# Four graph-attention layers by gathered rows: weights in PSUM, row sums on TensorE, heavy tiles first

## The chip, the cores and the metric

One NeuronCore of a Trainium2 chip runs the whole program. The metric is the device time of one execution in microseconds (us). Below, PE or TensorE is the matmul engine, DVE or VectorE the vector engine, ACT or ScalarE the activation engine, POOL or GpSimd the engine that issues the indirect gathers, and SP the engine that issues most plain DMAs.

## What is computed

The input is `x`, 4096 nodes by 256 features in float32, and `adj`, a symmetric 4096 x 4096 matrix of 0 and 1 with ones on the diagonal (a node has about eight neighbours besides itself, at most 23). Four layers follow each other:

```python
for layer in (L0, L1, L2, L3):
    h = maximum(layernorm(x), 0)
    x = x + layer(h, adj, weights)
```

Layers 0 and 2 are attention with 4 heads: a projection `Wh = h @ W`, a score `leaky_relu(s_i + s_j)` for each pair of neighbours, a softmax over a node's neighbours, and the weighted sum of the neighbours' rows of `Wh` (layer 0 applies ELU to it). Layer 1 has one head, weighs the rows of `h` itself and adds `h @ W`. Layer 3 is attention by dot products of a query with the neighbours' keys, 4 heads of 64, and sums their values.

## The kernel before

The kernel first reads `adj` (the "look"): TensorE packs each column's ones into words, DVE decodes them into a list of at most 23 neighbours per node, and the nodes are sorted by their number of neighbours. Sorted, they form `T = 32` tiles of 128 nodes; in tile `t` no node has more than `KS[t]` neighbours besides itself, from 23 in tile 0 to 3 in tile 31. The sum of `KS` is 276. If the graph doesn't fit, a general path (`Dense`) would run, and it doesn't here.

A layer then runs over the 32 tiles in the order `ORDER`: 31, 29, ..., 1, 0, 2, ..., 30, so that light tiles stand at both ends. For each tile

- POOL (`gp_gather`) issues `KS[t]` indirect gathers, each of which fetches one neighbour's table row for the 128 nodes of the tile from HBM (1 KB, in layer 3 2 KB) into a slot of `s_ring`; SP (`sp_own`) loads the node's own row. `s_ring` has `FLOATS = 28000` floats a partition, and its places are given at build time: `after[n]` says how many tiles of this layer must have been summed (`agg`) before tile n may be written. Gathers of layers 0 to 2 are also held to `PACE = 11` tiles ahead of the projection;
- DVE (`vec_scores`, in layer 3 `vec_dots`) makes the scores, ACT (`act_exp`) the exponentials and their sums, DVE divides (`vec_normal`), multiplies all slots by their weights (`vec_weigh`, L1278) and adds the slots up (`vec_sum`, L1286, a reduction over a strided view). In layer 3 ACT does three of the slots (`act_spare`);
- DVE adds the sum to `s_xs` (`vec_finish`) and takes mean and variance (`vec_stats`). ACT takes the root (`act_root`, L830), DVE the reciprocal and the product with the mean (`vec_norm`), ACT makes the next layer's hidden row (`act_hidden`, L843), TensorE transposes it (`pe_hidden`, L1423), ACT copies it out of PSUM (`act_turned`, L852), TensorE projects it (`pe_project`, L1443 to L1453), and ACT writes the row of the next layer's table (`act_row`) to HBM.

The next layer's first gather waits for every row of that table. In layer 3 there is no next table; POOL instead scatters each finished tile to the output (`gp_home`, L729), seven tiles behind the gathers. All waits are on semaphores that are counted; every engine runs its instructions in the order in which its method emits them:

```python
        if L.n < 3:
            for n in range(T):
                self.pe_hidden(e, L.n + 1, n)
                self.pe_project(e, L.n + 1, n)
```

On DVE the order is weigh n, norm n-1, scores n+1, sum n, finish n, stats n, normal n+1.

## Time and profile before

| | |
|---|---|
| time of a run, median of 3 | 2163.33 us (2163.15 to 2164.61) |
| profiled execution, its span | 2212.0 us |
| DVE busy in it | 1549.9 us (70%) |
| POOL busy | 1372.2 us (62%) |
| ScalarE busy | 811.5 us (37%) |
| TensorE busy with matmuls | 559.5 us (25%), mean granted clock 0.545 of full speed |
| the look and the sorting, before the first gather | 280.6 us |

The span reaches from the first to the last instruction of the profiled execution, a run of its own, which took longer than the three timed ones. Busy time counts an engine's own instructions, without waits and without the issuing of DMAs, save for the indirect ones, which POOL makes itself.

### The profile page before, as it was taken

To read this page: it belongs to the slowest core of one execution; us is meant where nothing else is said; L and a number is where in the kernel's file an instruction comes from. 1 tells how busy PE (TensorE), PEld (TensorE's weight loads), DVE (VectorE), ACT (ScalarE), POOL (GpSimd) and SP (SyncE) were. 2 spreads that over 40 slices of the span, in tenths; PEclk is the share of its full clock that TensorE was granted. 3 is DMA by queue.
4 is the path that set the end of the run, shared out by engine and by line. 5 is a ranking of instruction groups with operands and counts; after the bars stand their busy time and mean duration, and the time that the engine had idled before them with its cause. 6 is when DMAs were issued, how large, how long until landed. Compare 5 with 4: busy or idle time off the path is not lost.

```text
span 2212.0 us, 11389 instructions
## 1 busy us (share of the span) xinstructions
PE 559.5 (25%) x2091; PEld 280.8 (13%) x2092; DVE 1549.9 (70%) x2500; ACT 811.5 (37%) x2030; POOL 1372.2 (62%) x1200
## 2 busy tenths in 40 slices
PE   3565101221223232122343215545552000000000
PEld 2434000110111111011121102212220000000000
DVE  3878423999888677477875327897654987459897
ACT  6877002553456333113343214434443321102233
POOL 0000576788774777878737767887305788547885
PEclk9755555555555555555555556666665555555555
DMA  9996483444442444344425434444205665445663
GB/s 375 405 367 238 167 213 102 116 102 99 107 110 69 133 117 115 102 105 110 113 64 156 118 104 119 127 122 131 78 28 187 198 180 161 132 110 174 187 198 101
DMA packets 171382, 328.55 MB, mean 149 GB/s; under 512 B 40094, under 2 KB 83111, under 8 KB 171304
## 3 DMA queue, kind: packets, MB, share of 16 engines
q0 software_dynamic: 65920, 197.88, 33.1%
q1 hardware_dynamic: 82600, 104.48, 13.9%
q10 hardware_dynamic: 22784, 25.40, 3.3%
q14 instruction: 59, 0.48, 0.1%
q8 instruction: 19, 0.31, 0.1%
HBM read 288.94 MB, written 38.72 MB: 148 GB/s over the span
## 4 chain that ended last, share of the span: by engine, by line
POOL 36%; issue 23%; ACT 12%; DVE 11%; PE 10%; another core or an unknown queue 5%; DMA 2%; ACTq 1%; SPq 1%; POOLq 0%; DVEq 0%
POOL s_ring L722 35%; DVE s_y L1286 5%; PE ps L1443 3%; ACT s_a L768 2%; PE ps L1412 2%; ACT L887 2%; ACT s_pr L887 2%; PE ps L1447 2%; DMA s_ring<-s_tab,s_idx 1%; DVE s_ring L1278 1%; DVE s_sc L1221 1%; DVE s_ring L1219 1%; POOL out_dram L729 1%; ACT s_hb L843 1%
## 5 line engine op out<-in xcount | busy, mean ns | idle before, releaser
L722 POOL DMA_INDIRECT s_ring<-s_tab,s_idx x1104 | 1297.2, 1175 | 571.5 <-issue 334.4
L1286 DVE TENSOR_REDUCE s_y<-s_ring 128x256 f32<-128x2048 f32 (+12 forms) x128 | 566.9, 4429 | 2.4 <-ACT s_ring L907 2.4
L1278 DVE TENSOR_TENSOR s_ring<-s_ring,s_pr 128x1792 f32<-128x1792 f32 (+14 forms) x128 | 323.4, 2526 | 3.4
L887 ACT ACTIVATE s_pr<-s_sc,s_least 128x8 f32<-128x8 f32 (+12 forms) x416 | 124.2, 301 | 413.4 <-DVE s_least L1225 261.1
L1451 PE MATMUL ps<-s_wx,s_hT 128*128 128x258 f32 (+1 forms) x256 | 134.8, 682 | 199.3 <-ACT s_hT L852 104.0
L709 POOL DMA_INDIRECT s_pay<-s_pay_t,s_rank_i x32 | 30.9, 966 | 238.3 <-DVE s_rank_i L1083 228.9
L1219 DVE TENSOR_TENSOR s_ring<-s_ring 128x2304 f32<-128x2304 f32 (+12 forms) x32 | 87.1, 2722 | 114.8 <-DMA s_ring<-s_tab,s_idx 114.7
L1423 PE MATMUL ps<-s_ident,s_hb 128*128 128x128 f32 x128 | 44.1, 448 | 437.7 <-ACT s_hb L843 319.5
L989 DVE RECIPROCAL s_stat<-s_stat 128x1 f32<-128x1 f32 x96 | 15.2, 159 | 188.4 <-issue 95.5
L830 ACT ACT_TABLE_LOAD x94 | 120.6, 1283 | 63.1 <-issue 35.9
L907 ACT ACTIVATE s_ring<-s_ring,s_pr 128x64 f32<-128x64 f32 x384 | 95.2, 334 | 120.8 <-issue 64.8
L887 ACT ACT_TABLE_LOAD x94 | 120.6, 1283 | 47.5 <-issue 45.2
L1443 PE MATMUL ps<-s_wx,s_hT 128*128 128x512 f32 x128 | 120.5, 1097 | 67.3 <-ACT s_hT L852 46.7
L768 ACT ACTIVATE s_a<-s_adj 128x4096 fp8e4<-128x4096 int32 x32 | 115.4, 3606 | 12.9 <-DMA s_adj<-in_adj_dram 12.9
L869 ACT ACTIVATE s_tb<-ps 128x256 f32<-128x256 f32 x32 | 12.3, 384 | 262.3 <-PE ps L1448 145.2
L1451 PEld LDWEIGHTS ps<-s_wx,s_hT 128*128 128x128 f32 x256 | 75.1, 324 | 237.4 <-ACT s_hT L852 122.4
L1423 PE MATMUL ps<-s_ident,s_tb 128*128 128x128 f32 x64 | 22.0, 448 | 272.2 <-ACT s_tb L843 195.6
L1205 DVE SCALAR_TENSOR_TENSOR s_sc<-s_ring 128x24 f32<-128x24 f32 (+16 forms) x96 | 18.2, 190 | 100.6 <-DMA s_ring<-s_tab,s_idx 100.2
L1221 DVE TENSOR_REDUCE s_sc<-s_ring 128x36 f32<-128x2304 f32 (+12 forms) x32 | 87.0, 2720 | 1.1
L1423 PEld LDWEIGHTS ps<-s_ident,s_hb 128*128 128x128 f32 x128 | 18.6, 204 | 467.5 <-ACT s_hb L843 346.4
L887 ACT ACTIVATION_READ_ACCUMULATOR s_pr<-s_sc,s_least 128x1 f32 x416 | 77.7, 187 | 0.0
L843 ACT ACTIVATE s_hb<-s_xs,s_stat 128x256 f32<-128x256 f32 x64 | 38.4, 600 | 98.8 <-DVE s_stat L991 82.1
(163 smaller groups left out, 1186.7 us busy)
## 6 DMA issues: line engine op xcount, KB each, us to landing
s_adj<-in_adj_dram SPq DMA_DIRECT2D x32, 2048.0 KB, 14.6
s_ring<-s_tab,s_idx POOLq DMA_INDIRECT x1104
s_tab<-s_tb ACTq DMA_DIRECT2D x32, 256.0 KB
s_ring<-s_tab SPq DMA_DIRECT2D x32, 256.0 KB
s_ring<-s_pay SPq DMA_DIRECT2D x32, 132.0 KB
s_tab<-s_tb ACTq DMA_DIRECT2D x32, 132.0 KB
s_ring<-s_tab SPq DMA_DIRECT2D x32, 132.0 KB
s_tab<-s_pay_t ACTq DMA_DIRECT2D x16, 260.0 KB, 6.5
```

The source lines that it names most:

```text
L722: e.indirect_dma_start(g[:, k, 0:L.row], None, self.tab_d[L.n], bass.IndirectOffsetOnAxis(ap=self.idx[:, t, k:k + 1], axis=0)).then_inc(se ...
L768: e.activation(self.a8[:, q % 2], self.adj[:, r], ACT.Copy, saturate=False).then_inc(self.conv)
L830: e.activation(st[:, 9:10], st[:, 8:9], ACT.Sqrt).then_inc(self.rooted)
L887: m = e.activation(p[:, :, h], s[:, :, h], ACT.Exp, bias=self.least[:, j, h:h + 1], scale=-1.0, accum_out=self.total[:, j, h:h + 1])
L907: m = e.activation(v, v, ACT.Copy, scale=p[:, k, h:h + 1])
L1219: e.tensor_tensor(keys, keys, wide(self.query(n), 1, k + 1), ALU.mult).then_inc(self.v)
L1221: e.tensor_reduce(s, keys.rearrange("p k (h d) -> p k h d", h=4), AX, ALU.add).then_inc(self.v)
L1278: e.tensor_tensor(g, g, wide(p[:, a:], 3, L.hd), ALU.mult).then_inc(self.weighed)
L1286: e.tensor_reduce(self.y[:, n % 2, :], g[:, :, v0:v0 + D].rearrange("p k d -> p d k"), AX, ALU.add).then_inc(self.agg)
L1423: x = e.transpose(self.bank(self.turn_bank(n), P * k, P), h[:, P * k:P * k + P], self.ident[:])
L1443: e.matmul(o, self.hT[:, j, k, :], self.wx[:, k, D:3 * D], start=(k == 0), stop=False)
L1451: x = e.matmul(o[:, 0:cols], self.hT[:, j, k, :], self.wx[:, k, 0:cols], start=(k == 0), stop=(k == 1 and l == 1))
```

## The change

- The ring is laid out once for all four layers (`lay_ring`), with 30100 floats; `agg` counts on over the layers. `PACE` goes. A ring place may be reused once seven tiles, or those that overlap it, are summed.
- Layers 0 to 2 take the tiles heavy ones first (`DOWN`), layer 3 in a written order (`MIXED`).
- The softmax weights `p` are written to PSUM (banks 0 and 1) and read there by `vec_normal` and `vec_weigh`; ACT copies layer 3's query to PSUM (`act_asked`), where `vec_dots` reads it. The weights of the three slots that ACT does are kept in SBUF (`few`).
- `vec_sum` goes. `pe_sum` adds the weighed slots up in PSUM by identity matmuls, in two pieces that `vec_weigh` releases one after the other. TensorE takes the transposes and the projection of tile n-1, then the sum of tile n.
- Layer 1 multiplies by the reciprocal of the sum of weights in `vec_finish`, behind the sum.
- `act_root` and `vec_norm` go; `act_scale` makes the reciprocal root as exp(-0.5 ln(variance + eps)) on ACT, and the product with the mean there too. A table set with both functions is loaded ahead of a layer.
- The neighbours' table rows of a tile are put in order while layer 0 runs (`vec_places`, in place of a copy), tables of layers 1 to 3 begin one row later, and POOL could issue some gathers of the first tiles when all rows but the last four tiles' have landed. How many is in `EARLY`, which is empty for all layers: POOL waits for all rows of the table, and then issues the layer's first gather.

The core of the diff:

```diff
-ORDER = tuple(range(T - 1, 0, -2)) + tuple(range(0, T, 2))
+DOWN = tuple(range(T))
+MIXED = (5, 6, 7, 8, 31, 28, 0, 11, 17, 29, 24, 10, 4, 9, 26, 18, 1, 3, 16, 14, 21, 13, 30, 2, 20, 12, 19, 27, 15, 25, 22, 23)
 PAY = 2 * D + 8 + SLOTS
-FLOATS = 28000
-PACE = 11
+FLOATS = 30100
 SPARED = 3
+LATE = 4
+SOON = 1 + P * (T - LATE)
+EARLY = ((), (), (), ())
...
+def lay_ring():
+
+    spans, at = [], 0
+    for L in LAYERS:
+        for t in L.order:
+            size = (KS[t] + 1) * L.slot + (D if L.n == 3 else 0)
             at = 0 if at + size > FLOATS else at
-            past = [k + 1 for k, (a, b) in enumerate(spans) if a < at + size and b > at]
-            self.after.append(max(past + [m - 7, 0]))
-            self.at.append(at)
...
+            self.em, self.few = s2("em", [P, 2, D]), s2("few", [P, 2, SPARED, 4])
+            self.sc = s2("sc", [P, 2, 4 * SLOTS])
...
+    def total_y(self, n):
+        return self.bank(2 + n % 2, 0, D)
...
+        part = lambda a: a[:, 0:k * H].rearrange("p (k h) -> p k h", h=H)
+        return part(self.sc[:, n % 2, :]), part(self.bank(n % 2, 0, 96))
...
+    def gp_gather(self, e, L, n, a, b):
+        t = L.order[n]
         g = self.rows(L, n)
+        early = b < KS[t]
         if L.n == 0:
-            e.wait_ge(self.listed, 4 - t // 8)
-        if L.after[n]:
-            e.wait_ge(self.agg, T * L.n + L.after[n])
-        if L.n < 3 and n > PACE:
-            e.wait_ge(self.projected, T * (L.n + 1) + n - PACE)
-        for k in range(KS[t]):
-            e.indirect_dma_start(g[:, k, 0:L.row], None, self.tab_d[L.n],
+            e.wait_ge(self.listed, t // 8 + 1)
+        if a == 0 and L.after[n]:
+            e.wait_ge(self.agg, L.after[n])
+        table = self.tab_d[L.n][0:SOON, :] if early else self.tab_d[L.n]
+        for k in range(a, b):
+            e.indirect_dma_start(g[:, k, 0:L.row], None, table,
                                  bass.IndirectOffsetOnAxis(ap=self.idx[:, t, k:k + 1], axis=0)).then_inc(self.gat[n % 8], 16)
...
+            for n in range(soon):
+                if L.n == 1:
+                    e.wait_ge(self.sorted, n + 1)
+                self.gp_gather(e, L, n, 0, EARLY[L.n][n])
+            for j in range(4):
+                e.wait_ge(self.tab_out[j], self.stored(L.n, T - 4 + j))
+            if L.n == 1:
+                e.wait_ge(self.sorted, T)
         for n in range(T):
-            self.gp_gather(e, L, n)
+            self.gp_gather(e, L, n, EARLY[L.n][n] if n < soon else 0, KS[L.order[n]])
...
+    def act_scale(self, e, l, n):
+
+        st, a = self.stat[:, 16 * (n % 2):16 * (n % 2) + 16], self.as_
+        e.wait_ge(self.var_ok, self.norms(l, n) + 1)
+        e.activation(st[:, 8:9], st[:, 7:8], ACT.Ln, bias=self.eps[:]).then_inc(self.a)
+        e.wait_ge(self.a, a.up())
+        e.activation(st[:, 10:11], st[:, 8:9], ACT.Exp, scale=-0.5).then_inc(self.a)
+        e.wait_ge(self.a, a.up())
+        e.activation(st[:, 11:12], st[:, 12:13], ACT.Copy, scale=st[:, 10:11]).then_inc(self.a)
+        e.wait_ge(self.a, a.up())
+
+    def act_hidden(self, e, l, n):
+
         st = self.stat[:, 16 * (n % 2):16 * (n % 2) + 16]
-        e.wait_ge(self.var_ok, self.norms(l, n) + 1)
-        e.activation(st[:, 9:10], st[:, 8:9], ACT.Sqrt).then_inc(self.rooted)
-
-    def act_hidden(self, e, l, n):
-
-        st = self.stat[:, 16 * (n % 2):16 * (n % 2) + 16]
-        e.wait_ge(self.normed, self.norms(l, n) + 1)
+        self.act_scale(e, l, n)
...
+    def act_asked(self, e, n):
+
+        L = LAYERS[3]
+        e.wait_ge(self.own_in[n % 8], self.own_landed(L, n))
+        if n > 1:
+            e.wait_ge(self.scored, 3 * T + n - 1)
+        e.activation(self.asked_for(n), self.query(n), ACT.Copy).then_inc(self.asked)
...
+        e.preload_act_table_set("natural_log_exp_and_others")
+        if l == 1:
+            e.wait_ge(self.ruled, 3 + len(set(KS)))
+        if l == 4:
+            self.act_asked(e, 0)
+            self.act_asked(e, 1)
         for n in range(T):
+            if n and l == 1:
+                self.act_below(e, n - 1)
+            self.act_exp(e, L, n)
             if l == 4:
-                self.act_spare(e, n)
-                if n + 1 < T:
-                    self.act_exp(e, L, n + 1)
-                continue
-            if n:
+                if n + 2 < T:
+                    self.act_asked(e, n + 2)
+                if n:
+                    self.act_spare(e, n - 1)
+            elif n:
                 self.act_hidden(e, l, n - 1)
-            if n + 1 < T:
-                self.act_exp(e, L, n + 1)
-            if n:
                 self.act_turned(e, l, n - 1)
-            if l == 1:
-                self.act_below(e, n)
-            if n:
                 self.act_row(e, l, n - 1)
-            self.act_root(e, l, n)
+        if l == 1:
+            self.act_below(e, T - 1)
         if l < 4:
             self.act_hidden(e, l, T - 1)
-            self.act_table(e, l, T - 1)
+            self.act_turned(e, l, T - 1)
+            self.act_row(e, l, T - 1)
+        else:
+            self.act_spare(e, T - 1)
...
-        e.tensor_scalar(st[:, 8:9], st[:, 7:8], EPS, None, ALU.add).then_inc(self.var_ok)
-
-    def vec_norm(self, e, l, n):
-        vs, st = self.vs, self.stat[:, 16 * (n % 2):16 * (n % 2) + 16]
-        e.wait_ge(self.rooted, self.norms(l, n) + 1)
-        e.wait_ge(self.hidden, T * l + n - 1)
-        e.reciprocal(st[:, 10:11], st[:, 9:10]).then_inc(self.v)
-        e.wait_ge(self.v, vs.up())
-        e.scalar_tensor_tensor(st[:, 11:12], st[:, 6:7], -1.0, st[:, 10:11], ALU.mult, ALU.mult).then_inc(self.normed)
+        e.tensor_scalar(st[:, 12:13], st[:, 6:7], -1.0, None, ALU.mult).then_inc(self.var_ok)
...
+    def vec_places(self, e, n):
+
+
+        vs, k = self.vs, KS[n]
+        m = -(-k // 8) * 8
+        found, values, to = self.place[:], self.hits[:, n, 0:m], self.met_at[:, 0:k]
+        e.tensor_copy(self.hits[:, n, 0:k], self.rows(LAYERS[0], n)[:, 0:k, D + 4]).then_inc(self.v)
+        e.wait_ge(self.v, vs.up())
+        for a in range(0, m, 8):
+            if a:
+                e.match_replace(values, found[:, a - 8:a], values, 0.0).then_inc(self.v)
+                e.wait_ge(self.v, vs.up())
+            e.max(found[:, a:a + 8], values).then_inc(self.v)
+            e.wait_ge(self.v, vs.up())
+        e.tensor_scalar(to, found[:, 0:k], 0.0, float(N + 1), ALU.is_gt, ALU.mult).then_inc(self.v)
+        e.wait_ge(self.v, vs.up())
+        c = self.soonest(n)
+        if c:
+            e.tensor_tensor(to, to, found[:, 0:k], ALU.subtract).then_inc(self.v)
+            e.wait_ge(self.v, vs.up())
+            e.tensor_scalar(self.over[:, n, 0:c], to[:, 0:c], float(SOON - 1), 0.0, ALU.subtract, ALU.max).then_inc(self.v)
+            e.wait_ge(self.v, vs.up())
+            e.tensor_scalar(to[:, 0:c], to[:, 0:c], float(SOON - 1), None, ALU.min).then_inc(self.v)
+            e.wait_ge(self.v, vs.up())
+            e.tensor_copy(self.idx[:, n, 0:k], to).then_inc(self.sorted)
+        else:
+            e.tensor_tensor(self.idx[:, n, 0:k], to, found[:, 0:k], ALU.subtract).then_inc(self.sorted)
...
+    def pieces(self, L, n):
+
+        a, b = SPARED if L.n == 3 else 0, KS[L.order[n]] + 1
+        c = (a + b + 1) // 2
+        return [(a, c), (c, b)] if c < b else [(a, b)]
 
     def vec_weigh(self, e, L, n):
 
         H, v0 = L.heads, D if L.n == 3 else 0
-        a = SPARED if L.n == 3 else 0
-        p = self.scores(L, n)[1]
-        g = self.rows(L, n)[:, a:, v0:v0 + D].rearrange("p k (h d) -> p k h d", h=H)
-        e.wait_ge(self.normal, T * L.n + n + 1)
-        e.tensor_tensor(g, g, wide(p[:, a:], 3, L.hd), ALU.mult).then_inc(self.weighed)
-
-    def vec_sum(self, e, L, n):
-
-        v0, g = D if L.n == 3 else 0, self.rows(L, n)
-        e.wait_ge(self.weighed, T * L.n + n + 1)
-        if L.n == 3:
-            e.wait_ge(self.spared, n + 1)
-        e.tensor_reduce(self.y[:, n % 2, :], g[:, :, v0:v0 + D].rearrange("p k d -> p d k"), AX, ALU.add).then_inc(self.agg)
+        p, parts = self.scores(L, n)[1], self.pieces(L, n)
+        if L.n == 1:
+            e.wait_ge(self.p_ok, T + n + 1)
+        else:
+            e.wait_ge(self.normal, self.normals(L, n))
+        for a, b in parts:
+            g = self.rows(L, n)[:, a:b, v0:v0 + D].rearrange("p k (h d) -> p k h d", h=H)
+            e.tensor_tensor(g, g, wide(p[:, a:b], 3, L.hd), ALU.mult).then_inc(self.weighed, 2 // len(parts))
...
+        self.vec_weights(e, LAYERS[l])
         for n in range(T):
+            self.vec_scores(e, L, n)
+            if L.n == 0:
+                self.vec_places(e, n)
+            if L.n == 1:
+                self.vec_mutual(e, n)
+            if n:
+                self.vec_finish(e, L, n - 1)
+                self.vec_stats(e, l, n - 1)
+            if L.n == 0 and n > 1:
+                self.vec_apart(e, n - 2)
+            self.vec_normal(e, L, n)
             self.vec_weigh(e, L, n)
...
+    def pe_sum(self, e, L, n):
+
+        g, y, g0 = self.rows(L, n), self.total_y(n), T * L.n + n
+        v0, b = D if L.n == 3 else 0, KS[L.order[n]] + 1
+        parts = self.pieces(L, n)
+        if g0 > 1:
+            e.wait_ge(self.x_new, g0 - 1)
+        for i, (a, c) in enumerate(parts):
+            e.wait_ge(self.weighed, 2 * g0 + (i + 1) * (2 // len(parts)))
+            for k in range(a, c):
+                x = e.matmul(y, self.ident[:], g[:, k, v0:v0 + D], start=(k == parts[0][0]), stop=(k == b - 1 and L.n < 3))
+        if L.n == 3:
+            e.wait_ge(self.spared, n + 1)
+            for k in range(SPARED):
+                x = e.matmul(y, self.ident[:], g[:, k, v0:v0 + D], start=False, stop=(k == SPARED - 1))
+        x.then_inc(self.agg)
+
     def pe_layer(self, e, L):
+        l = L.n + 1
         if L.n == 2:
             e.wait_ge(self.missed_ok, 1)
-            e.matmul(self.bank(0, 0, 1)[0:1, :], self.missed[:, 0:1], self.ones[:, 0:1], start=True,
+            e.matmul(self.bank(4, 0, 1)[0:1, :], self.missed[:, 0:1], self.ones[:, 0:1], start=True,
                      stop=True).then_inc(self.met_sum)
             e.wait_ge(self.sym_ok, 1)
-        if L.n < 3:
-            for n in range(T):
-                self.pe_hidden(e, L.n + 1, n)
-                self.pe_project(e, L.n + 1, n)
+        for n in range(T):
+            if n and l < 4:
+                self.pe_hidden(e, l, n - 1)
+                self.pe_project(e, l, n - 1)
+            self.pe_sum(e, L, n)
```

## Rows read from the trace of the kernel before

**Rows 1.** The page: busy time of each engine, and the gathers' group.

```profile
PE 559.5 (25%) x2091; PEld 280.8 (13%) x2092; DVE 1549.9 (70%) x2500; ACT 811.5 (37%) x2030; POOL 1372.2 (62%) x1200
...
L722 POOL DMA_INDIRECT s_ring<-s_tab,s_idx x1104 | 1297.2, 1175 | 571.5 <-issue 334.4
```

**Rows 2.** Windows by layer: length; busy PE, PEld, DVE, ACT, POOL; clock, DMA, GB/s.

```profile
280.60:724.80 444.20, 88.81 (x192) 46.85 (x192) 335.95 (x524) 187.40 (x512) 319.61 (x277) 0.50 0.45 114
724.80:1161.50 436.70, 127.79 (x258) 62.82 (x258) 318.32 (x494) 139.24 (x254) 322.73 (x276) 0.50 0.41 109
1161.50:1678.20 516.70, 218.49 (x384) 87.26 (x384) 308.75 (x421) 183.26 (x478) 315.41 (x277) 0.61 0.39 107
1678.20:2212.00 533.80, 0.00 (x0) 0.00 (x0) 408.44 (x288) 136.22 (x640) 379.00 (x308) 0.50 0.57 167
```

**Rows 3.** Timeline of a heavy tile, layer 2: start, length.

```profile
1440.80 6.56 DVE L1278 TENSOR_TENSOR s_ring<-s_ring,s_pr 128x6144 f32<-128x6144 f32 x1
...
1441.37 6.81 POOL L722 DMA_INDIRECT s_ring<-s_tab,s_idx  x1 [0.30 <-issue]
...
1448.21 11.17 DVE L1286 TENSOR_REDUCE s_y<-s_ring 128x256 f32<-128x6144 f32 x1
...
1449.72 0.95 POOL L722 DMA_INDIRECT s_ring<-s_tab,s_idx  x1 [0.30 <-issue]
```

**Rows 4.** Waits in layer 2, 1213 to 1330 us: total, times, longest.

```profile
ACT s_tb L869 <- remote: 85.4, 4, 25.6
```

**Rows 5.** Groups by line: the reduction over a tile's rows.

```profile
L1286 DVE TENSOR_REDUCE s_y<-s_ring 128x256 f32<-128x2048 f32 (+12 forms) x128 | 566.9, 4429 | 2.4 <-ACT s_ring L907 2.4
```

**Rows 6.** Narrow stretches of TensorE's timeline, read for their starts.

```profile
1473.64 1.06 PE L1447 MATMUL ps<-s_wx,s_hT 128*128 128x256 f32 x2
...
1474.07 0.95 PE L1447 MATMUL ps<-s_wx,s_hT 128*128 128x256 f32 x2
...
1455.28 0.59 PE L1447 MATMUL ps<-s_wx,s_hT 128*128 128x256 f32 x2
...
1455.49 0.59 PE L1447 MATMUL ps<-s_wx,s_hT 128*128 128x256 f32 x2
```

**Rows 7.** Timeline of the last tiles of layer 1.

```profile
1149.11 0.42 DVE L1300 TENSOR_TENSOR s_xs<-s_xs,s_y 128x256 f32<-128x256 f32 x1
...
1150.25 0.15 DVE L983 TENSOR_SCALAR s_stat<-s_stat 128x1 f32<-128x1 f32 x1
...
1152.80 0.20 ACT L830 ACTIVATE s_stat<-s_stat 128x1 f32<-128x1 f32 x1 [0.40 <-ACT s_tb L866]
...
1153.43 0.60 ACT L843 ACTIVATE s_hb<-s_xs,s_stat 128x256 f32<-128x256 f32 x1 [0.42 <-DVE s_stat L991]
...
1154.08 0.69 PE L1423 MATMUL ps<-s_ident,s_hb 128*128 128x128 f32 x2 [2.11 <-ACT s_hb L843]
...
1155.24 2.13 PE L1451 MATMUL ps<-s_wx,s_hT 128*128 128x264 f32 x4 [0.47 <-ACT s_hT L852]
...
1157.30 1.24 PE L1453 MATMUL ps<-s_bx,s_ones 1*128 1x264 f32 x2
```

**Rows 8.** Timeline of layer 0, act_below's second operation.

```profile
698.67 0.42 ACT L897 ACTIVATE s_em<-s_em 128x256 f32<-128x256 f32 x1
```

**Rows 9.** Windows of TensorE in layer 2's projections: length, busy, clock.

```profile
1451.20:1454.30 3.10, 3.10 (x4) 0.50 0.44 117
1454.30:1457.80 3.50, 2.00 (x7) 0.99 0.39 103
1457.80:1465.90 8.10, 0.00 (x0) 0.50 0.49 143
1468.80:1474.80 6.00, 5.99 (x9) 0.50 0.51 138
```

**Rows 10.** Chain that ended last, a landing in layer 3: start, length.

```profile
1889.35 4.12 DMA s_ring<-s_tab,s_idx
```

**Rows 11.** The page: loads of ScalarE's tables ahead of the root.

```profile
L830 ACT ACT_TABLE_LOAD x94 | 120.6, 1283 | 63.1 <-issue 35.9
```

More of the change, by code:

```diff
@@ L536, in query, with asked_for @@
         L = LAYERS[3]
-        a = L.at[n] + (KS[ORDER[n]] + 1) * L.slot
+        a = L.at[n] + (KS[L.order[n]] + 1) * L.slot
         return self.ring[:, a:a + D]
+    def asked_for(self, n):
+        return self.bank(4 if n % 2 == 0 else 6, 0, D)
+    def total_y(self, n):
+        return self.bank(2 + n % 2, 0, D)
     def landed(self, L, n):
-        every = lambda c: sum(KS[ORDER[m]] for m in range(c) if m % 8 == n % 8)
-        return 16 * (L.n * every(T) + every(n + 1))
+        every = lambda M, c: sum(KS[M.order[m]] for m in range(c) if m % 8 == n % 8)
+        return 16 * (sum(every(M, T) for M in LAYERS[0:L.n]) + every(L, n + 1))
     def own_landed(self, L, n):
@@ L842, in act_hidden @@
             h = self.hb[:, n % 2, :]
[L843 removed]
+        e.activation(h, self.xs[:, n, :], ACT.Relu, bias=st[:, 11:12], scale=st[:, 10:11]).then_inc(self.hidden)
     def act_turned(self, e, l, n):
@@ L1183, in vec_lists @@
         vs = self.vs
-        for g in (3, 2, 1, 0):
+        for g in range(4):
             part = slice(8 * g, 8 * g + 8)
```

238 lines of the change are left out of this document (122 added, 116 removed).

## Prediction

> **What bounds the kernel now.** I read the page first. VectorE (DVE) is busy 1549.9 us of 2212.0 and GpSimd (POOL) 1372.2 us, of which 1297.2 us are the 1104 indirect gathers of L722 [rows 1]. The two are close, so I cut the trace where each layer's first gather starts: layers 0 to 3 last 444.2, 436.7, 516.7 and 533.8 us behind a beginning of 280.6 us [rows 2]. In no layer is an engine busy all the time: POOL works 72, 74, 61 and 71% of them, DVE 76, 73, 60 and 77%.
>
> Next I looked at single gathers. An undisturbed one takes 0.95 us and 0.30 us pass to the next, so 1.25 us each. Where the weighing multiply L1278 runs, one gather lasts as long as the multiply: 6.81 us beside 6.56 us. The reduction of 11.17 us behind it holds no gather back [rows 3]. Undisturbed, 276 gathers of a layer need 276 x 1.25 = 345 us. Against 1104 x 0.95 = 1049 us, the 1297.2 us [rows 1] hold 248 us of such holds.
>
> The Trainium skill ("SBUF — State Buffer", Who interferes with whom) says that a `tensor_tensor` with two SBUF inputs takes only the shared read interface and was not seen to stall DMA, since descriptor generation needs the write interface. By that page the move of the weights to PSUM would free nothing; the measured 6.81 us speak against it, and I go by them.
>
> Third, the profiled execution is 48.7 us longer than the median of 2163.33 us. In layer 2, four times, ScalarE waited for something unknown, 85.4 us in all [rows 4], between projections that otherwise follow each other evenly. The gathers ran ahead and took up part of that loss. I place the 48.7 us there, so that layer 2 has 468.0 us in a timed run: 280.6 + 444.2 + 436.7 + 468.0 + 533.8 = 2163.3. My sum is made without such a stall, so it stands against the median; made against 2212.0 it would have 48.7 us more.
>
> **The change part by part.**
> *Weights in PSUM.* `p` and layer 3's query are read from PSUM, so the big multiplies have one SBUF input, as has the reduction, which holds nothing [rows 3]. I take the holds as gone. In layer 3 POOL is busy 379.0 us [rows 2]; 276 gathers and 32 scatters, taken as long as a gather, at 0.95 us would be 292.6, so 86 us go. If the hold stays, nothing goes: both ends are kept.
>
> *Sums on TensorE.* L1286 leaves DVE: 566.9 us, 4.43 us a tile [rows 5]. In its place come 276 + 32 = 308 identity matmuls of 256 columns a layer, each as two instructions. Two such are 0.43 us apart at a granted clock of 0.50 and 0.21 us apart at 1.00 [rows 6]: 0.854 or 0.427 us a slot, 263 or 132 us a layer. DVE then has slack everywhere. TensorE is not hidden, because `pe_layer` now puts transposes and projection of tile n-1 before the sum of tile n. That closes a ring: sum n-1, finish and statistics on DVE, scale and hidden on ScalarE, transposes, copy, projection, sum n.
>
> *The ring, from rows.* From L1300's start (1149.11) to L983's end (1150.40) 1.3 us. The three small ScalarE operations that replace root, reciprocal and product are new; each is like L830, 0.20 us and a handoff of 0.04, so 0.7 us. Hidden 0.60 and handoff: 0.65. From the transposes (1154.08) to the projection (1155.24) 1.2 us [rows 7]. With handoffs F = 4.0 us in layers 1 and 2. Layer 0 adds `act_below`, two operations of 0.42 us with handoffs, and a second DVE operation as long [rows 8]: F = 5.4 us. The small three are bounded by nothing (0) and by 0.60 us each, as L843 (+1.1 us); their form is L830's, so I take 0.7. The projection P at the low clock: 2.1 us for layer 0; 3.3 us in layer 1 with the bias (1155.24 to 1158.54) [rows 7]; for layer 3's weights 5.99 us within the stretch and a little behind it, 6.3 [rows 9].
>
> *The clock.* In the projections of layer 2, TensorE worked from 1451.2 at 0.50 and the clock rose at 1454.3, after 3.1 us of work; in the next round it was still low after 6.0 us. With little work behind the rise it was low again from 1457.8 [rows 9]. So I take the low level (1.2 GHz) for the first 4.5 us of each burst of projection and sum, the middle of the two, and 2.4 GHz behind it: a burst is 4.5 + (P + 0.854 s - 4.5)/2 for s slots, and a round, with 0.15 us of drain, is F + 2.4 + P/2 + 0.427 s. That gives 8.8, 8.0 and 9.6 us + 0.427 s in layers 0, 1 and 2. A mean tile (s = 9.6) needs 12.9, 12.1 and 13.7 us; its gathers 8.6 x 1.25 = 10.8 us. The ring is the new bound, not POOL.
>
> The Trainium skill ("TensorE: Matmul & The Clock Gate", HAM oscillation) says that gaps between bursts return the array to half rate, so that every burst starts cold; the trace agrees.
>
> *Heavy tiles first.* The first tiles have gathers longer than a round (23, 14, 13 gathers: 28.8, 17.5, 16.3 us); behind these the rounds count. Layer 0: tiles 0 to 4, 74 gathers, 92.5 us; 5.6 us for landing and scores; 28 rounds from tile 4 on, 28 x 8.8 + 0.427 x 242 = 349.7; the last tile's way to the next layer's first gather, F + P and 3.0 us (1158.54 to 1161.5 [rows 2, 7]), 10.5: 458. Layer 1: 96 gathers 120; 5.6; 26 x 8.0 + 0.427 x 217 = 300.7; 10.3: 437. Layer 2: 62 gathers 77.5; 5.6; 29 x 9.6 + 0.427 x 255 = 387.3; 14.6 with longer copies: 485. The 5.6 is an estimate: 4.1 us from a tile's last gather to its landing [rows 10] and 1.5 us for three short score operations and an exponential. DVE's start in layer 0 falls within the 28.8 us of tile 0's gathers.
>
> *Layer 3.* No projection, so no ring. DVE does about 9 us a tile, TensorE 4.1 to 8.2. POOL is the bound: 345 us of gathers, 25 scatters between them at 0.95 + 0.30, 32 us; then the last tile and its scatter, about 20 us; 5 us for waits on room in the ring of 30100 floats. 402 us, against 533.8.
>
> *Costed at nothing.* `vec_places` (four to eight short operations a tile) and the exponentials run while TensorE sums; if that cover were gone, about 1.3 us a tile in layer 0, 40 us. The wait for all table rows, on POOL ahead of the whole layer, is there before too; `EARLY` is empty, so the sorted lists bring nothing. Table loads (L830: 94 of 1.283 us [rows 11], as many at L887) go; before they stood mostly beside DVE's reduction.
>
> *Sum.* 280.6 + 458 + 437 + 485 + 402 = 2063 us. Layers 0 to 2 together lose 31 us against 1348.9, layer 3 gains 132. I round to **2060 us**, 4.8% less.
>
> **Rivals.**
> *Clock stays low.* If bursts never raise it, the round is F + P + 0.15 + 0.854 s, 7.6, 7.4 and 10.4 us + 0.854 s. All 32 tiles then follow the ring: with 263 us of sums, the first tile's gathers and the way out, layers of about 553, 546 and 646 us, 2430 us in all. Against: the clock rises in bursts of 6 us [rows 9], and these are longer. It decides from 1.25 us a round on: 83 rounds x 1.25 = 103 us, my whole gain. This is the rival on the other side.
> *Clock stays high through the gaps.* Rounds of 6.6, 5.8 and 7.3 us + 0.427 s equal the gathers' pace, layers of about 390, 381 and 409: 1860 us. Against: it fell in the round shown [rows 9], and the gap stays at 3 to 4 us.
> *Gathers still held.* Then layer 3 keeps its 86 us and the first tiles of the others some 45 more: 2190 us, slower. For it speaks that the multiply still writes the ring; against it, that the reduction, with one SBUF input, held nothing. The page's rule above would have the same effect, by another cause.
> *Table loads within the ring.* If logarithm and exponential each load their own table, 2 x 1.283 us [rows 11] x 83 rounds = 213 us: 2275 us. The change preloads a set with both, so this is unlikely.
> *A slower ring.* Each of about ten handoffs 0.05 to 0.1 us dearer gives 0.5 to 1 us a round: 2100 to 2145 us.
>
> **How the numbers follow.** Forecast with its own range (2005 to 2095) 0.63; slower ring 0.16; clock high 0.08; clock low 0.04; gathers held 0.04; table loads 0.03; the change does nothing 0.02. A result under 0.2% (4 us), about what a measurement of this kernel can tell, counts as the same. Faster 0.87, same 0.02, slower 0.11. For 8 in 10 I take the forecast, the slower ring and a part of clock high: 1975 to 2150 us.
>
> **What would show it.** Gathers at 1.25 us also beside L1278's successor; no reduction of 4.4 us on DVE; TensorE about 1000 us busy, its clock changing once per round; in layers 0 to 2 rounds of 12 to 14 us with POOL waiting for the sum; the layers at 458, 437, 485, 402 us. Wrong, if the bursts are cut into pieces too short for the clock, if gathers are late by DMA in layer 3 (it would move about 220 GB/s where it moved 167 [rows 2]), or if ScalarE's order puts an exponential between statistics and hidden.

## The result, and the profile after

The changed kernel takes 2128.99 us (median of 4 runs, 2128.65 to 2130.79), the kernel before 2163.97 beside it (2163.15 to 2166.78). The ratio is 0.984, 95% interval 0.983 to 0.985: 1.6% or 35 us faster, where 103 were forecast. The profiled execution took 2128.94 us, 1.7 of them outside its span of 2127.2, and has no stall of the kind that [rows 4] show, so it stands against the median as it is.

Groups of the page of the changed kernel (line, engine, operation, count, then busy us and mean ns, idle time before):

```profile
PE 1221.5 (57%) x4555; PEld 834.4 (39%) x4556; DVE 991.3 (47%) x2452; ACT 645.3 (30%) x2069; POOL 1113.2 (52%) x1201
...
L746 POOL DMA_INDIRECT s_ring<-s_tab,s_idx x1104 | 1045.9, 947 | 740.9 <-issue 329.9
L1552 PE MATMUL ps<-s_ring,s_ident 128*128 128x256 f32 x2272 | 670.6, 461 | 380.6 <-DVE s_ring L1372 380.6
...
L864 ACT ACTIVATE s_stat<-s_stat,s_eps 128x1 f32<-128x1 f32 x96 | 28.3, 295 | 299.2 <-DVE s_stat L1033 299.2
```

POOL's gathers fell from 1297.2 us to 1045.9, 0.947 us each, so the holds of [rows 1, 3] are gone. DVE fell from 1549.9 to 991.3 us busy. The new work is on PE, busy for 1221.5 us where the prediction said about 1000. Windows from each layer's first gather to the next (first and last us, length, busy us of PE, PEld, DVE, ACT, POOL with instructions, granted clock, DMA share, GB/s):

```profile
283.50:751.50 468.00, 254.94 (x808) 193.41 (x808) 209.31 (x602) 126.86 (x513) 261.76 (x276) 0.74 0.44 110
751.50:1236.70 485.20, 331.12 (x874) 223.59 (x874) 171.80 (x400) 83.27 (x257) 261.28 (x277) 0.68 0.38 99
1236.70:1714.00 477.30, 324.04 (x1000) 188.67 (x1000) 157.75 (x357) 127.32 (x482) 261.49 (x276) 0.82 0.42 116
1714.00:2127.20 413.20, 186.43 (x616) 144.75 (x616) 273.29 (x319) 142.30 (x672) 293.06 (x308) 0.71 0.71 213
```

Against 458, 437, 485 and 402 us of the forecast, layer 1 stands out: 48 us longer, at the lowest clock. Against [rows 2], with layer 2 at 468.0 as in the prediction, layers 0 to 2 lost 24, 49 and 9 us and layer 3 gained 121.

The rounds are best read from TensorE. A round goes from the transposes of one tile to those of the next, and has one sum in it. From the transposes of tile 4 to those of tile 30 there are 26 rounds, with the sums of tiles 5 to 30, in each of layers 0 to 2:

```profile
413.60:734.50 320.90, 196.04 (x607) 147.66 (x607) 156.18 (x468) 101.70 (x416) 163.09 (x172) 0.77 0.35 93
871.20:1216.80 345.60, 256.15 (x659) 171.05 (x659) 124.62 (x314) 66.59 (x208) 170.56 (x181) 0.69 0.34 93
1352.70:1691.60 338.90, 251.09 (x762) 142.75 (x762) 117.43 (x288) 101.96 (x390) 173.50 (x184) 0.85 0.41 117
```

That is 12.34, 13.29 and 13.03 us a round. The forecast's formula gives, at their mean of 8.65 slots, 12.5, 11.7 and 13.3: right in layers 0 and 2, 1.6 us short in layer 1. One round of layer 1 on PE's timeline (start, length, operation, count, idle time before and what ended it), and its stretches as windows:

```profile
1087.52 0.69 PE L1508 MATMUL ps<-s_ident,s_hb 128*128 128x128 f32 x2 [2.97 <-ACT s_hb L882]
1088.68 2.13 PE L1537 MATMUL ps<-s_wx,s_hT 128*128 128x264 f32 x4 [0.47 <-ACT s_hT L891]
1090.74 1.24 PE L1539 MATMUL ps<-s_bx,s_ones 1*128 1x264 f32 x2
1091.92 6.30 PE L1552 MATMUL ps<-s_ring,s_ident 128*128 128x256 f32 x16
1101.18 0.47 PE L1508 MATMUL ps<-s_ident,s_hb 128*128 128x128 f32 x1 [2.96 <-ACT s_hb L882]
```

```profile
1087.50:1092.00 4.50, 4.00 (x9) 2.04 (x9) 1.84 (x6) 0.38 (x1) 2.68 (x3) 0.50 0.44 116
1092.00:1097.20 5.20, 5.20 (x13) 4.13 (x14) 0.00 (x0) 0.79 (x3) 0.00 (x0) 0.50 0.09 32
1097.20:1100.60 3.40, 1.02 (x5) 0.57 (x3) 2.20 (x6) 0.86 (x4) 1.80 (x2) 1.00 0.27 64
```

The idle gap ahead of the transposes is 2.97 us, and the projection ends 4.5 us behind their start, both as forecast. But the clock stands at 0.50 through 9.7 us of burst and rises when the sum is all but done. Over the 26 rounds it rose, where it rose within a burst, 8.4 us (median) behind the first transpose in layer 1 and 5.4 us in layer 0. One instruction in this list is unlike all others: L1539, the bias, `1*128`, over one partition. Layer 0 has no bias. The first experiment tests this.

### The profile page after: what moved, and what is told of

Read it like the earlier page. It is cut to its first block, busy times and chain, and to the rows that moved or that the text cites. A ratio compares the mean times of both kernels' runs of the same rounds, so it can differ in the third digit from the quotient of the medians.

```text
span 2127.2 us, 16493 instructions
## 1 busy us (share of the span) xinstructions
PE 1221.5 (57%) x4555; PEld 834.4 (39%) x4556; DVE 991.3 (47%) x2452; ACT 645.3 (30%) x2069; POOL 1113.2 (52%) x1201
## 4 chain that ended last, share of the span: by engine, by line
PE 47%; POOL 14%; ACT 14%; DVE 10%; issue 8%; DMA 4%; SPq 3%; ACTq 0%; DVEq 0%; POOLq 0%
PE ps L1552 25%; POOL s_ring L746 12%; PE ps L1537 6%; PE ps L1528 5%; PE ps L1508 3%; SPq L596 3%; ACT s_a L801 2%; PE ps L1497 2%; DVE s_stat L1028 2%; PE ps L1533 2%; ACT s_hb L882 2%; PE ps L1539 2%; ACT s_hT L891 2%; DMA s_ring<-s_tab,s_idx 2%; DMA s_adj<-in_adj_dram 1%
## 5 line engine op out<-in xcount | busy, mean ns | idle before, releaser
L746 POOL DMA_INDIRECT s_ring<-s_tab,s_idx x1104 | 1045.9, 947 | 740.9 <-issue 329.9
L1552 PE MATMUL ps<-s_ring,s_ident 128*128 128x256 f32 x2272 | 670.6, 461 | 380.6 <-DVE s_ring L1372 380.6
L1552 PEld LDWEIGHTS ps<-s_ring,s_ident 128*128 128x128 f32 x2272 | 532.7, 239 | 516.7 <-issue 332.5
L1372 DVE TENSOR_TENSOR s_ring<-s_ring,ps 128x1280 f32<-128x1280 f32 (+8 forms) x255 | 330.9, 1339 | 4.5
L926 ACT ACTIVATE ps<-s_sc,s_least 128x9 f32<-128x9 f32 (+12 forms) x416 | 109.6, 264 | 482.4 <-DVE s_least L1273 254.0
L1267 DVE TENSOR_TENSOR s_ring<-s_ring,ps 128x2304 f32<-128x2304 f32 (+12 forms) x32 | 87.1, 2721 | 125.6 <-DMA s_ring<-s_tab,s_idx 125.3
L864 ACT ACTIVATE s_stat<-s_stat,s_eps 128x1 f32<-128x1 f32 x96 | 28.3, 295 | 299.2 <-DVE s_stat L1033 299.2
L954 ACT ACTIVATE s_ring<-s_ring,s_few 128x64 f32<-128x64 f32 x384 | 94.6, 333 | 0.0
L926 ACT ACTIVATION_READ_ACCUMULATOR ps<-s_sc,s_least 128x1 f32 x416 | 77.6, 186 | 0.0
L1497 PE MATMUL ps<-s_wx,s_hT 128*128 128x264 f32 x128 | 67.3, 681 | 17.2 <-ACT s_pay_t L855 16.5
```

The lines of the kernel that those rows point to most:

```text
L746: e.indirect_dma_start(g[:, k, 0:L.row], None, table, bass.IndirectOffsetOnAxis(ap=self.idx[:, t, k:k + 1], axis=0)).then_inc(self.gat[n % ...
L926: m = e.activation(p[:, :, h], s[:, :, h], ACT.Exp, bias=self.least[:, j, h:h + 1], scale=-1.0, accum_out=self.total[:, j, h:h + 1])
L954: m = e.activation(v, v, ACT.Copy, scale=p[:, k, h:h + 1])
L1267: e.tensor_tensor(keys, keys, wide(self.asked_for(n), 1, k + 1), ALU.mult).then_inc(self.v)
L1372: e.tensor_tensor(g, g, wide(p[:, a:b], 3, L.hd), ALU.mult).then_inc(self.weighed, 2 // len(parts))
L1497: x = e.matmul(self.bank(7, 0, cols), self.hT[:, t % 2, k, :], self.wx[:, k, 0:cols], start=(k == 0), stop=(k == 1))
```

## The experiments

All change `after` (the changed kernel) unless said, and the diffs show the core of each edit. Times are medians of four runs. The ratios are to the kernel before, measured beside them on the same chip: 2162.4 us beside e1, e2, e5 and e6, 2162.94 beside e3, e4, e7 and e8; for the other runs it stands with them. Theory A and theory B are the two that each expectation sets against each other.

**Run e1, the bias over 128 partitions.** `bx` gets 128 partitions, with zeros in all but the first (cleared once, in the beginning):

```diff
-            x = e.matmul(o[:, 0:cols], self.ones[0:1, :], self.bx[0:1, 0:cols], start=False, stop=True)
+            x = e.matmul(o[:, 0:cols], self.ones[:], self.bx[:, 0:cols], start=False, stop=True)
```

> The changed kernel, with one thing different in layer 1 (the projections of its tiles, for layer 2's table): the bias is added by a matmul over 128 partitions (ones times a matrix whose rows below the first are zero) where it is a matmul over one partition; same columns, same values, same number of instructions. In the trace of the changed kernel layer 1's rounds average 13.29 us over tiles 5 to 30 at a sum of 0.730 us a slot, layer 0's 0.582. Theory A, the one-partition matmul of 1.1 us in the middle of layer 1's burst keeps the granted clock from rising: with 128 partitions the sums of layer 1 fall to about layer 0's 0.58 us a slot, some 1.3 us a round, so layer 1 lasts about 450 instead of 485.2 us and the whole 2095. Theory B, the clock depends on the time that TensorE is at work or on the idle gap alone: nothing changes, 2129 within 4 us.

Measured: 2062.02 us, ratio 0.953 (0.951 to 0.955). Layer 1, and one of its rounds of the same 16 sum instructions:

```profile
750.10:1169.70 419.60, 260.18 (x874) 198.67 (x874) 172.19 (x400) 83.19 (x257) 261.41 (x276) 0.77 0.43 114
```

```profile
1050.88 0.44 PE L1511 MATMUL ps<-s_ident,s_hb 128*128 128x128 f32 x2 [2.97 <-ACT s_hb L884]
1051.79 2.12 PE L1540 MATMUL ps<-s_wx,s_hT 128*128 128x264 f32 x4 [0.47 <-ACT s_hT L893]
1053.71 1.08 PE L1542 MATMUL ps<-s_bx,s_ones 128*128 128x264 f32 x2
1054.60 3.72 PE L1555 MATMUL ps<-s_ring,s_ident 128*128 128x256 f32 x16
```

The sum takes 3.72 us for 6.30. Layer 1 went from 485.2 to 419.6 us; layers 0 and 2 stayed, 466.7 for 468.0 and 481.4 for 477.3. Theory A holds, more strongly than expected (30 us more): rounds of 11.04 us, the rise 4.5 us (median) behind the first transpose.

**Runs e10 and e11, the same in layer 0.** A matmul of no use behind each projection, over one partition in e10 and over 128 in e11:

```diff
+                if l == 1:
+                    e.matmul(self.bank(2 + (n + 1) % 2, D, D), self.ones[0:1, :], self.wx[0:1, 0, 0:D], start=True, stop=True)
```

> The changed kernel, with a matmul of no use behind each projection of layer 0 (256 columns, into a part of a bank that nothing reads), over one partition, as layer 1's bias is. Layer 0 has no such matmul now and lasts 468.0 us at 0.582 us a slot. Theory A, a one-partition matmul between projection and sum keeps the granted clock from rising: layer 0's rounds become layer 1's 13.29 plus the longer gap of 1.36 us, 14.65 where they are 12.34, some 70 us more; 2200 in all. Theory B, the clock follows the time at work, whatever the rows: the 1.1 us of work at 0.50 costs at most that a round, 0 to 34 us: 2129 to 2163, and the same as its twin over 128 partitions.

> As the run before, but the matmul of no use in layer 0 is over 128 partitions. Theory A: it counts as work, so that the rise comes no later than now and the matmul pays part of itself: 11.04 plus 1.36 us, 12.4 a round, layer 0 at 465 to 485 us and the whole at 2126 to 2146. Theory B: as its twin over one partition.

Measured: 2528.22 and 2470.77 us, beside 2214.16 for the kernel before (2188.92 to 2227.65). On this chip the engines waited for things that the trace calls remote, which means that it has no name for them, in e10 DVE alone for 256.3 us at one line. In layers 0 to 2 the transposes behind the first sum came 76 to 78 us after it, where 3 to 4.3 are usual. So the totals can't be used. The rounds behind can: layers 1 and 2, which the edit leaves alone, have 13.25 and 13.00 us here, for 13.29 and 13.03 in the changed kernel. Layer 0's 26 rounds, in e10 and then e11:

```profile
502.70:881.80 379.10, 254.24 (x658) 170.84 (x658) 155.92 (x468) 101.71 (x416) 122.26 (x129) 0.70 0.24 64
```

```profile
494.60:827.60 333.00, 208.08 (x659) 158.26 (x659) 155.86 (x468) 101.72 (x416) 122.29 (x129) 0.77 0.28 73
```

14.58 us with one partition (14.65 expected), 12.81 with 128 (12.4), 12.34 without either. The same columns cost 2.2 us a round over one partition and 0.5 us over 128; the rise came at 8.0 and 5.6 us. Theory A.

**Run e2, the gap filled.**

```diff
+            if l < 4 and n < T - 1:
+                for _ in range(17 if l == 1 else 11):
+                    e.matmul(self.bank(2 + (n + 1) % 2, D, P), self.ident[:], self.ones[:], start=True, stop=True)
```

> The changed kernel, with matmuls of no use (128 columns, into a part of a PSUM bank that nothing reads) behind each sum of layers 0 to 2, 17 of them in layer 0 and 11 in layers 1 and 2, so that TensorE is at work through the 4.33 us and the 2.97 and 2.90 us in which it now waits for VectorE and ScalarE. Theory A, the low granted clock after each gap is what makes the rounds 12.3, 13.3 and 13.0 us: without gaps it stays at 1.00, a burst costs half, the rounds fall below the pace of the gathers (1.25 us each) and the layers to about 390, 385 and 410 us: 1880 in all. Theory B, the gap isn't what lowers it (it falls for another reason): the added work of 2.4 and 3.7 us at the high clock takes 4.8 and 7.3 us at the low one, 2 to 3 us longer than the gaps, and the kernel is slower, about 2300.

Measured: 1928.96 us, ratio 0.891 (0.888 to 0.894).

```profile
283.60:684.10 400.50, 306.84 (x1862) 271.37 (x1862) 211.11 (x602) 126.99 (x513) 261.78 (x276) 0.91 0.51 129
684.10:1087.60 403.50, 316.83 (x1556) 251.31 (x1556) 172.07 (x400) 83.20 (x257) 260.97 (x276) 0.87 0.45 119
1087.60:1514.60 427.00, 347.61 (x1682) 253.28 (x1682) 158.47 (x357) 127.02 (x482) 261.64 (x276) 0.94 0.47 130
```

Theory A: more work on TensorE, 200 us less. Rounds fell to 10.24, 10.50 and 11.34 us. The run is 49 us slower than the 1880 of theory A: even at the high clock a round takes longer than the gathers of a mean tile, 9.6 us (7.65 of them of 1.25 us). The Trainium skill ("TensorE: Matmul & The Clock Gate", HAM oscillation) says that gaps return the array to half rate; this run, in which they are down to 0.5 us, agrees (clock 0.99 in layer 0's rounds and 1.00 in layer 2's). In layer 1 it was 0.95 in the projections and 0.89 in the sums, so that a gap isn't the only thing.

**Run e8, filler and bias over 128 partitions** (both edits).

> The run with filler matmuls, and the bias of layer 1's projections over 128 partitions. With filler the granted clock was 0.94 and 0.89 in layer 1's projections and sums and 0.99 to 1.00 in layers 0 and 2: its layer 1 lasted 403.5 us. Theory A, the one-partition matmul is what still makes the clock fall there: with 128 partitions it is above 0.98 throughout and layer 1 lasts 380 to 392, in all about 1912. Theory B, the falls in layer 1 have another cause: 1929 within 5 us.

Measured: 1913.55 us, ratio 0.884 (0.882 to 0.887). Layer 1 fell to 388.4 us and its rounds from 10.50 to 10.01 us. That is theory A in the time (380 to 392 us, 1912 in all). In the clock it is so for the sums alone, 0.98 for 0.89; in the projections the clock was 0.91 for 0.95, where theory A had above 0.98 throughout. Why it still falls in some rounds there stays open.

**Run e5, weights in PSUM alone.** An edit of the kernel before (one small sum moves to another bank to make room):

```diff
-        return [a[:, n % 2, 0:k * H].rearrange("p (k h) -> p k h", h=H) for a in (self.sc, self.pr)]
+        part = lambda a: a[:, 0:k * H].rearrange("p (k h) -> p k h", h=H)
+        return part(self.sc[:, n % 2]), part(self.bank(n % 2, 0, 96) if L.n < 3 else self.pr[:, n % 2])
```

> The kernel before, with one part of the change alone: in layers 0 to 2 the softmax weights are in PSUM; sums stay on VectorE, order, norms and layer 3 as before. Theory A (mine of the prediction): the weighing multiply with one SBUF input holds no gather, so the 58.7, 62.0 and 54.6 us by which the gathers of layers 0 to 2 exceed 0.945 us each go to under 2 us each; but POOL waits there for room and for its pace already, so that the time falls by less than the 175 us in all: between 0 and 120, I take 2100. Rival B: the holds come from the write into the ring and stay: 2163 within 4 us, layer excess 50 us or more.

Measured: 2053.08 us, ratio 0.949 (0.947 to 0.951), where the expectation took 2100 in a range down to 2043: 109 us faster, three times the gain of the whole change. Its layers, and its gathers in layer 3, where the weights are still in SBUF:

```profile
280.90:675.70 394.80, 88.83 (x192) 46.88 (x192) 334.81 (x524) 187.61 (x512) 262.09 (x276) 0.50 0.50 128
675.70:1060.30 384.60, 127.75 (x258) 62.91 (x258) 317.62 (x494) 139.18 (x254) 261.59 (x277) 0.50 0.47 123
1060.30:1518.00 457.70, 222.03 (x384) 88.92 (x384) 308.82 (x421) 182.99 (x478) 262.39 (x277) 0.62 0.44 121
1518.00:2052.30 534.30, 0.00 (x0) 0.00 (x0) 408.40 (x288) 136.22 (x640) 377.05 (x308) 0.50 0.57 167
```

```profile
L723 POOL DMA_INDIRECT s_ring<-s_tab,s_idx x276 | 336.9, 1221 | 237.7 <-DMA s_q<-s_tb 111.5 <-issue 82.9 <-DVE s_y L1287 43.3
```

A gather takes 0.95 us in layers 0 to 2, where it took 1.16, 1.17 and 1.14 in the kernel before (the busy times of [rows 2] by 276), and 1.221 in layer 3, which the edit leaves alone. In layers 0 to 2 the multiply writes the ring in both kernels; what differs is where the weights, its second input, lie. That is the hold, and rival B is out. The remark of the Trainium skill weighed in the prediction ("SBUF — State Buffer", Who interferes with whom), that a `tensor_tensor` with two SBUF inputs was not seen to stall DMA, is not borne out. The same section says that an instruction of DVE with two SBUF inputs contends with one of GpSimd that reads SBUF; the gathers read their row numbers (`s_idx`) there, and these times agree with that. The prediction weighed the remark alone.

**Run e6, sums back on VectorE.** `pe_sum` isn't called; behind each `vec_weigh`:

```diff
+        e.tensor_reduce(self.total_y(n), g[:, :, v0:v0 + D].rearrange("p k d -> p d k"), AX, ALU.add).then_inc(self.agg)
```

> The changed kernel with one part undone: VectorE sums a tile's slots by one reduction (into the same PSUM bank), TensorE does the transposes and projections alone; all else is as changed. VectorE then has 4.4 us a tile more, 142 us a layer, beside the 209, 172, 158 and 273 us that it is busy now; TensorE's burst is the projection alone, off the way from one sum to the next. Theory A, the ring through TensorE at its half clock is the bound of the changed kernel: without it layers 0 to 2 last what VectorE or the gathers need, 400 to 430 us each, layer 3 the sum on VectorE 415 to 450, in all 1990 to 2060, faster than the changed kernel. Theory B, moving the sums was worth its while: VectorE is the bound again, layers 0 to 2 at 440 and more and layer 3 at 480, 2160 to 2200.

Measured: 2037.31 us, ratio 0.942 (0.939 to 0.944).

```profile
282.60:704.70 422.10, 88.78 (x192) 46.85 (x192) 353.88 (x634) 126.83 (x513) 262.14 (x277) 0.50 0.49 122
704.70:1082.60 377.90, 127.77 (x258) 62.85 (x258) 308.76 (x432) 82.89 (x257) 261.17 (x277) 0.50 0.48 126
1082.60:1513.40 430.80, 194.78 (x384) 77.83 (x384) 303.73 (x389) 123.85 (x482) 261.74 (x276) 0.65 0.46 128
1513.40:2035.80 522.40, 0.00 (x0) 0.00 (x0) 409.85 (x351) 142.37 (x672) 293.03 (x308) 0.50 0.56 168
```

Theory A in the total and nearly in layers 0 to 2 (400 to 430 each; layer 1 took less); but layer 3 lasted 522.4 us and not 415 to 450. Against the changed kernel, with layers of 468.0, 485.2, 477.3 and 413.2 us, summing on TensorE costs 46, 107 and 47 us in layers 0 to 2 and gives 109 in layer 3.

**Run e7, TensorE sums layer 3 alone.** As e6, with `if L.n == 3` ahead of the call of `pe_sum`.

> The changed kernel with its sums on TensorE in layer 3 alone; in layers 0 to 2 VectorE sums, as in the run with all sums on VectorE. Theory A, the effects of the layers add: 282.6 + 422.1 + 377.9 + 430.8 from that run and 413.2 from the changed kernel, 1927 within 8 us. Rival, layer 3 profits from TensorE's clock or the state of the ring left by the layers before, so that it needs up to 20 us more behind sums on VectorE: 1945.

Measured: 1927.98 us, ratio 0.892 (0.890 to 0.893); layers of 421.6, 378.0, 430.8 and 411.9 us. The layers add up.

**Run e3, the sum ahead of the projection.** No work is added or left out; VectorE and ScalarE are put in the matching order, and the sums of the weights get a third buffer:

```diff
         for n in range(T):
+            self.pe_sum(e, L, n)
             if n and l < 4:
                 self.pe_hidden(e, l, n - 1)
                 self.pe_project(e, l, n - 1)
-            self.pe_sum(e, L, n)
```

> The changed kernel with another order in layers 0 to 2, nothing added or left out: TensorE sums tile n before it turns and projects tile n-1; VectorE scores tile n+1 and weighs tile n ahead of finish and statistics of tile n-1; ScalarE takes the exponential of tile n+1 first. So the way from sum n-1 over statistics and hidden to the transposes lies beside sum n, and TensorE's idle gap of 2.9 to 4.3 us a round is gone. Theory A, the ring and its gap are the bound: the rounds fall below the gathers' pace of 1.25 us each and layers 0 to 2 last about 395, 385 and 410 us as with the filler matmuls (400.5, 403.5, 427.0), in all 1880 to 1930. Theory B, without filler the array has idle time again as soon as the gathers are the bound, the granted clock is low for most of a burst, and the bursts at 0.50 (3.25, 4.46, 7.4 us and 0.854 us a slot: 11.5, 12.7 and 15.6 us at 9.6 slots) are the new bound: 410, 430 and 500 us, about 2030.

Measured: 1882.51 us, ratio 0.871 (0.869 to 0.873).

```profile
282.60:679.20 396.60, 232.50 (x808) 178.39 (x808) 212.27 (x602) 126.74 (x513) 262.62 (x277) 0.77 0.51 130
679.20:1051.70 372.50, 251.01 (x874) 176.64 (x874) 171.15 (x400) 83.05 (x257) 261.38 (x276) 0.80 0.49 129
1051.70:1467.40 415.70, 297.14 (x1000) 179.20 (x1000) 159.13 (x357) 124.30 (x482) 261.44 (x276) 0.87 0.49 133
```

Theory A: 396.6, 372.5 and 415.7 us for 395, 385 and 410. Gathers follow each other without a pause, 344 to 345 us a layer; in layers 0 to 2 POOL waits only at their ends. The granted clock was 0.77, 0.80 and 0.87 there, so the gain isn't that of a high clock throughout: the way through the other engines now lies beside the sum. Which engine's order does how much was not taken apart.

**Run e4, e3 and the bias over 128 partitions.**

> The run with the sum first, and the bias of layer 1's projections over 128 partitions as in the first run. If the one-partition matmul acts only through the granted clock, and if in that order TensorE has no say in the round (theory A), nothing comes on top of the run with the sum first, within 6 us. If TensorE is the bound there (theory B), layer 1 gains 15 to 60 us, as it gained 65.6 in the ring.

Measured: 1882.1 us, ratio 0.870 (0.868 to 0.873), layer 1 371.6 us for 372.5. The 65.6 us that this edit gave in the ring are worth nothing once TensorE isn't the bound.

**Runs e9 and e12, early gathers.** e3 with

```diff
-EARLY = ((), (), (), ())
+EARLY = ((), (6, 5, 5, 4, 4), (6, 5, 5, 4, 4), (4, 4, 4, 3))
```

> The run with the sum first, and EARLY filled: in layers 1 and 2 the first 6, 5, 5, 4, 4 gathers of tiles 0 to 4, in layer 3 the first 4, 4, 4, 3 of its first four tiles, wait only for the table rows of tiles 0 to 27 (their lists are sorted, so that these take rows from there). In the run with the sum first POOL stood 51, 28 and 71 us between the last gather of one layer and the first of the next, and gathered without a pause otherwise. Theory A, these pauses are what stands above the 345 us of gathers now: 24, 24 and 15 gathers of 1.25 us move into them, 79 us in all, less what they bring forward too early: 1800 to 1830 us. Theory B, the wait for the last four tiles' rows costs little, since VectorE and TensorE have work from the layer before until then and tile 0 of the next can't be weighed earlier: within 10 us of 1882.

> The kernel of the run with early gathers once more, since in the call of that run all engines stood for long at things that the trace calls remote (the kernel before took 2189 to 2228 us there, where it takes 2163). Theory A, the pauses of POOL between layers (51, 28 and 71 us with the sum first) take in up to 24, 24 and 15 early gathers of 1.25 us: 1800 to 1830 us. Theory B, the first tile can't be weighed earlier anyway: within 10 us of 1882.

Measured: 2142.7 us in e9, ratio 0.973 (0.964 to 0.982), on the chip of e10 and e11 with its remote waits, which says little. The same kernel in e12: 1811.01 us beside 2164.8 for the kernel before, ratio 0.837 (0.834 to 0.839). POOL's waits for other engines and transfers in e3, without those of layer 3's scatters (us in total, times, longest); the first is ahead of the layers, the others lie between them:

```profile
POOL s_pay L733 <- DVE s_rank_f L1133: 230.6, 1, 230.6
POOL s_ring L746 <- DMA s_tab<-s_tb: 77.6, 2, 50.2
POOL s_ring L746 <- DMA s_q<-s_tb: 70.5, 1, 70.5
```

In e12 the pauses between the layers' gathers, from start to start, are 16, 7 and 30 us where they were 51, 28 and 71; behind the early gathers of layers 1 and 3 POOL waited another 4 and 23 us. Theory A. It is the fastest kernel here, 16% under the kernel before.

## Why the prediction was wrong, and where it was right

The direction and the structure were right, the size not: 35 us for 103. The forecast's 2063 misses the span of 2127.2 by 64. In the table, in us, "first tiles" is the time from a layer's first gather to the sum from which the forecast counts rounds (that of tile 4, 6 and 3 in layers 0, 1 and 2), and "way out" the time from the last sum to the next layer's first gather:

| | forecast | measured |
|---|---|---|
| beginning | 280.6 | 283.5 |
| layers 0, 1, 2: first tiles | 98.1, 125.6, 83.1 | 119.3, 138.1, 91.4 |
| layers 0, 1, 2: rounds | 349.7, 300.7, 387.3 | 337.1, 335.2, 372.6 |
| layers 0, 1, 2: way out | 10.5, 10.3, 14.6 | 11.6, 11.8, 13.3 |
| layer 3, to its last gather, and behind | 382, 20 | 380.7, 32.5 |

So the first tiles miss by 42 us, the rounds by 34 in layer 1 and by -13 and -15 in the others, and the end of layer 3 by 12.

**Right.** *Holds gone*: by the traces the gathers have 0.95 us everywhere, and e5 shows the second SBUF input to be the cause. *DVE with slack*, 4.4 us a tile gone. *The ring*: PE's gap (4.33, 2.97 and 2.90 us) and the stretch from transposes to projection (1.1, 1.0 and 1.0 on the mean) come out at F = 5.4, 4.0 and 3.9 us for 5.4, 4.0 and 4.0. The three small ScalarE operations took 0.29, 0.20 and 0.30 us, about 0.9 with their handoffs where 0.7 was taken, inside that sum. No table loads came into the rings. The low-clock projections are 2.1 and 3.3 us in layers 0 and 1, as taken; in layer 2 none ran at the low clock to its end (the longest, 6.3 us, at 0.54). `vec_places` stayed hidden: F didn't grow in layer 0, which has it.

**The step that failed** is "So I take the low level (1.2 GHz) for the first 4.5 us of each burst of projection and sum": one figure for three layers, from the projections of layer 2 [rows 9]. Counted from the projection's start, the rise came after 4.3, 7.5 and 3.9 us (medians) in layers 0, 1 and 2. In layer 1 a mean round has 4.0 us of F, 3.0 of projection and 6.3 of sum, 13.3 in all, and the sum cost 0.73 us a slot (0.58 in layer 0, 0.46 in layer 2). From tile 6's sum to the end of tile 31's, in the changed kernel and then in e1:

```profile
889.70:1224.90 335.20, 249.20 (x635) 166.09 (x634) 115.78 (x295) 64.42 (x201) 156.63 (x166) 0.69 0.33 89
```

```profile
881.60:1158.10 276.50, 190.12 (x635) 144.36 (x633) 117.36 (x300) 64.34 (x201) 161.69 (x171) 0.81 0.41 110
```

The forecast had 300.7 us for this stretch. e1 takes the loss away, and more: 59 us here and 65.6 in the layer, where the layer had missed by 48. e10 puts it into layer 0 and e11 does not: a matmul over one partition between projection and sum keeps the low clock. The bias instruction stands in [rows 7] as one of the operations on the way; I took its 1.1 us and not its one partition. That e1, at 2062.02 us, meets the forecast of 2063 is luck: its layers took 467, 420, 481 and 412 us for 458, 437, 485 and 402.

**A second term was mis-sized**, and over the whole kernel it weighs as much: the start of the first tiles, their gathers and then 5.6 us to the sum. In layer 0 the sum of tile 0 came 21 us late (next paragraph). In layers 1 and 2 the sum of tile 0 started 39.7 and 40.9 us into the layer and not 34.4 (28.8 + 5.6). The 5.6 us have no weighing in them, and TensorE waits for the first of its two pieces, 3.3 us in tile 0 of layer 1:

```profile
787.74 6.62 DVE L1372 TENSOR_TENSOR s_ring<-s_ring,ps 128x3072 f32<-128x3072 f32 x2
791.24 2.05 PE L1552 MATMUL ps<-s_ring,s_ident 128*128 128x256 f32 x4 [43.75 <-DVE s_ring L1372]
```

By tile 6's sum the delay in layer 1 was 12.5 us; in e1 it went from 5.4 to 5.9 only, so the growth is the one-partition bias again.

**Layer 0**, 468.0 for 458, is two misses of opposite sign: the sum of tile 4 started 119.3 us into the layer for 98.1, the rounds took 13 us less. VectorE began to score only at 332 us. Its row of the waits from 283 to 356 us:

```profile
DVE s_tmp L1009 <- DMA s_tmp<-in_L_gnn_a_dram: 41.5, 1, 41.5
```

It waited for a part of the next layer's weights; so "DVE's start in layer 0 falls within the 28.8 us of tile 0's gathers" was wrong. In the kernel before, VectorE stands at the same operation for 29.7 us (L960), which the prediction left out. **Layer 2**: in its sums the clock was at 1.00 throughout. **Layer 3**: POOL bounds it up to its last gather, as forecast; but the last tiles with their scatters took 32.5 us for "about 20".

**Rivals.** *Clock stays high through the gaps* was priced at 1860; e2 made it so at 1929. Of *clock stays low* some 40% came true in one layer (48 us of the 109 between its 546 and the forecast's 437), by a cause that I didn't have. *Gathers still held* and *table loads* are out, by the rows above. 2129 us lies within the 2100 to 2145 of *a slower ring*, and within the 1975 to 2150 given 8 in 10, but not for the reason given there: F was as forecast.

**Where the gain went.** e5 shows 109 us for the weights in PSUM of layers 0 to 2 alone. e6 against the changed kernel shows what the sums on TensorE cost and give: +200 in layers 0 to 2 and -109 in layer 3. The prediction had seen the ring as the new bound and counted a loss of 31 us in layers 0 to 2; it was 82, against what had been there before, holds included. The order of the engines' work, and the gap that it leaves on TensorE, is the root: e3, with the same operations in another order, gets back 246 us. How the remaining parts (heavy tiles first, one ring of 30100 floats, norms by logarithm) share in the rest was not taken apart.
